# A perceiver's cross-attention on one core: value and key fills interleaved, and the next batch's context turned one tile per piece

## The reference, cut to what matters

```python
x, ctx_1024: (8, 128, 512), (8, 2048, 512)      # 16 heads of 64
q = einsum('btd,dhk->bthk', layernorm(x), Wq) + bq
k = einsum('bsd,dhk->bshk', ctx_1024, Wk) + bk
v = einsum('bsd,dhk->bshk', ctx_1024, Wv) + bv
probs = softmax(einsum('bshk,bthk->bhts', k, q / 8), axis=-1)
attn = einsum('bhts,bshk->bthk', probs, v)
x = x + einsum('bthk,hkd->btd', attn, Wo) + bo
```

## Time and profile before

| | us |
|---|---|
| three timed runs | 3320.79, 3321.17, 3326.48 |
| their median | 3321.17 |
| the profiled execution | 3323.82 |
| its span, first to last instruction | 3322.1 |
| PE busy (share of the span) | 3094.8 (93%) |
| DVE busy | 1755.2 (53%) |
| ACT busy | 1453.4 (44%) |
| mean granted PE clock | 0.930 |

### The profile page before, as it was taken

One profiled execution on the slowest core, in us unless ns is written; L12 is line 12 of the kernel. 1 busy time (PEld: TensorE's weight loads), 2 busy tenths in 40 slices (PEclk: granted clock), 3 DMA queues, 4 the chain that ended last, 5 costly groups with the idle time before them and its releaser, 6 DMA issues. The chain is left out here.

```text
span 3322.1 us, 62803 instructions
## 1 busy us (share of the span) xinstructions
PE 3094.8 (93%) x25686; PEld 2701.5 (81%) x25686; DVE 1755.2 (53%) x3257; ACT 1453.4 (44%) x2994; POOL 116.5 (4%) x87
## 2 busy tenths in 40 slices
PE   6899999999999999999999999999879679869997
PEld 5688888888888888888888888888736579859997
DVE  5355656565565555556555555655523788740001
ACT  3355555555555555555555555555512510011111
POOL 0000000000000000000000000000040320100001
PEclk9899999999999999999999999999989755579998
DMA  7311221121121112112112111211080000217761
GB/s 304 118 40 38 74 63 45 55 76 38 51 74 57 42 57 67 38 51 74 57 44 67 57 51 44 74 43 38 10 192 7 16 33 0 78 50 275 252 238 59
DMA packets 234789, 253.16 MB, mean 76 GB/s; under 512 B 22296, under 2 KB 169912, under 8 KB 234064
## 3 DMA queue, kind: packets, MB, share of 16 engines
q1 hardware_dynamic: 233008, 241.79, 22.8%
q0 software_dynamic: 1280, 4.20, 0.4%
q10 hardware_dynamic: 288, 4.19, 0.3%
HBM read 215.42 MB, written 34.70 MB: 75 GB/s over the span
## 5 line engine op out<-in xcount | busy, mean ns | idle before, releaser
L216 PE MATMUL fills<-wv_group,ctxT_hi 128*128 128x256 f32 x4096 | 799.5, 288 | 1.3 <-DVE ctxT_lo L421 0.6
L224 PE MATMUL fills<-ctxT_hi,wk_pairs 128*128 128x512 f32 x2048 | 704.9, 405 | 0.7 <-DVE keys L436 0.7
L216 PEld LDWEIGHTS fills<-wv_group,ctxT_hi 128*128 128x128 f32 x4096 | 655.3, 191 | 24.2 <-issue 21.0
L436 DVE SCALAR_TENSOR_TENSOR keys<-fills,bk,keys 64x512 fp32r<-64x512 f32 x512 | 383.8, 750 | 412.1 <-ACT keys L353 408.4
L216 PE MATMUL fills<-wv_group,ctxT_lo 128*128 128x256 f32 x2048 | 579.4, 283 | 0.0
L353 ACT ACTIVATE keys<-fills,bk 64x512 fp32r<-64x512 f32 x512 | 350.0, 684 | 408.3 <-PE fills L224 405.0
L224 PEld LDWEIGHTS fills<-ctxT_hi,wk_pairs 128*128 128x128 f32 x2048 | 387.8, 189 | 103.7 <-issue 23.8
L429 DVE TENSOR_TENSOR values<-fills,values 128x512 fp32r<-128x512 f32 x256 | 176.9, 691 | 435.7 <-ACT values L348 435.7
L224 PE MATMUL fills<-ctxT_lo,wk_pairs 128*128 128x512 f32 x1024 | 403.5, 394 | 0.0
L216 PEld LDWEIGHTS fills<-wv_group,ctxT_lo 128*128 128x128 f32 x2048 | 392.7, 192 | 0.0
L473 DVE TENSOR_TENSOR probsT<-probsT_ps,probsT 128x512 fp32r<-128x512 f32 x504 | 348.3, 691 | 66.3 <-ACT probsT L385 57.1
(11 more groups left out here) (211 smaller groups left out, 3105.5 us busy)
## 6 DMA issues: line engine op xcount, KB each, us to landing
e_w<-in_L_ffn_W SPq DMA_DIRECT2D x64, 1024.0 KB, 8.7
ctx_stage<-in_ctx SPq DMA_DIRECT2D x128, 256.0 KB, 2.9
wv_group<-wv_split SPq DMA_DIRECT2D x64, 512.0 KB, 4.6
wk_pairs<-wk_split SPq DMA_DIRECT2D x128, 256.0 KB, 3.2
q<-q_split SPq DMA_DIRECT2D x256, 64.0 KB, 2.7
q_split<-p_qb SPq DMA_DIRECT2D x16, 512.0 KB, 3.5
o_parts<-o_half SPq DMA_DIRECT2D x128, 64.0 KB, 1.5
a_ua<-o_parts SPq DMA_DIRECT2D x32, 256.0 KB, 6.6
```

The lines of the kernel that those rows point to most:

```text
L216: last = nc.tensor.matmul(pJ[:, bank[0], 256 * k:256 * k + 256], c[:, t, s:s + P], wv[:, w, t, :], start=t + n == 0, stop=t == DT - 1 and ...
L224: last = nc.tensor.matmul(pJ[:, bank[0], :], wk[:, p, w, t, :], c[:, t, 512 * j:512 * j + 512], start=t + n == 0, stop=t == DT - 1 and n == 2)
L436: last = nc.vector.scalar_tensor_tensor(out=keys[lo_rows(j), x, 512 * j:512 * j + 512], in0=pJ[DK * a:DK * a + DK, bk_, :], scalar=bk_sb[h ...
```

## The change

A group's fills come in the order V V K V V K V V K V V K K K K K: value fills at positions 0, 1, 3, 4, 6, 7, 9, 10 (`VALUE_AT`), the first pair's key fills at 2, 5, 8, 11 and the second pair's at 12 to 15 (`KEY_AT`). The 16 context tiles of the next batch are turned in pieces 45 to 57 (`CTX_AT`): two in 45, 46 and 57, one in each of the ten between. A piece's first tile is at the piece's start, as before; a second one, where there is one, between the scores and the fill. Numbers, banks and waits follow from the new tables by the same rules. On SP, the value weights of the next group but one are loaded after position 11, right ahead of the first pair's key weights (before: after position 7), and each context tile is loaded alone, behind the fill that frees its buffer. No matmul, evacuation or DMA is added or removed.

```diff
-    FIRST_CTX = 47
+    VALUE_AT = (0, 1, 3, 4, 6, 7, 9, 10)
+    KEY_AT = ((2, 5, 8, 11), (12, 13, 14, 15))
+    CTX_AT = (45, 45, 46, 46, 47, 48, 49, 50, 51, 52, 53, 54, 55, 56, 57, 57)
+
+    def work_of(pos):
+        if pos in VALUE_AT:
+            return 0, VALUE_AT.index(pos)
+        p = pos in KEY_AT[1]
+        return 1 + p, KEY_AT[p].index(pos)
+
+    def turns(m):
+        return [u for u in range(ST) if CTX_AT[u] == m]
 
     def fill_no(m, last=False):
-        return m if last else m + 2 * min(max(m - FIRST_CTX + 1, 0), ST // 2)
+        return m if last else m + sum(at <= m for at in CTX_AT)
 
     def ctx_no(u):
-        return FIRST_CTX + 3 * (u // 2) + u % 2
+        return CTX_AT[u] + u
...
 # SP
-                            k = 16 * g + 4 * i + j - FIRST_CTX
-                            if not last and 0 <= k < (ST - NS) // 2:
-                                sp.wait_ge(filled, PRO + PER * b + ctx_no(2 * k + 1) + 1)
-                                ctx_load(sp, b + 1, 2 * k + NS)
-                                ctx_load(sp, b + 1, 2 * k + NS + 1)
+                            for u in () if last else turns(16 * g + 4 * i + j):
+                                if u + NS < ST:
+                                    sp.wait_ge(filled, PRO + PER * b + ctx_no(u) + 1)
+                                    ctx_load(sp, b + 1, u + NS)
...
-                        if i and not (last and g >= 2):
+                        if i >= 2 and not (last and g >= 2):
                             sp.wait_ge(filled, PRO + PER * b + fill_no(16 * g + 4 * i + 3) + 1)
-                            if i == 1:
+                            if i == 2:
                                 wv_load(sp, (g + 2) % XG)
-                            else:
-                                wk_load(sp, (g + 2) % XG, i - 2)
+                            wk_load(sp, (g + 2) % XG, i - 2)
...
 # PE
+            def fill(no, seq, pos):
+                kind, n = work_of(pos)
+                if n == 0:
+                    pe.wait_ge(wk_in[kind - 1] if kind else wv_in, 32 * seq + 32)
                 pe.wait_ge(fill_lo, no - 1)
-                if i < 2:
-                    v_fill(seq, j, i)
+                if kind:
+                    k_fill(kind - 1, n)
                 else:
-                    k_fill(i - 2, j)
+                    v_fill(n)
...
-                            if turn:
-                                bank[0] = ctx_no(2 * k) % 2
-                                ctx_fill(PRO + PER * b + ctx_no(2 * k), b + 1, 2 * k)
+                            new = [] if last else turns(m)
+                            for u in new[0:1]:
+                                bank[0] = ctx_no(u) % 2
+                                ctx_fill(PRO + PER * b + ctx_no(u), b + 1, u)
...
-                            if turn:
-                                bank[0] = ctx_no(2 * k + 1) % 2
-                                ctx_fill(PRO + PER * b + ctx_no(2 * k + 1), b + 1, 2 * k + 1)
+                            for u in new[1:2]:
+                                bank[0] = ctx_no(u) % 2
+                                ctx_fill(PRO + PER * b + ctx_no(u), b + 1, u)
...
 # ACT
-                                if g and i < 2 and j == 0:
+                                pos = 4 * i + j
+                                if g and pos == VALUE_AT[0]:
                                     act.wait_ge(weighed, 64 * b + 16 * g)
-                                if i >= 2 and j == 0:
-                                    act.wait_ge(scored, 16 * b + 4 * g + 2 * (i - 2) + 2)
+                                for p in range(2):
+                                    if pos == KEY_AT[p][0]:
+                                        act.wait_ge(scored, 16 * b + 4 * g + 2 * p + 2)
```

More of the change, by code:

```diff
@@ L43, in cross_attention, with through @@
     PIECES = 16 * XG
-    FIRST_CTX = 47
     PRO = ST + 16
     PER = PIECES + ST
+    VALUE_AT = (0, 1, 3, 4, 6, 7, 9, 10)
[8 more added lines that the diff above has]
+        return [u for u in range(ST) if CTX_AT[u] == m]
     def fill_no(m, last=False):
-        return m if last else m + 2 * min(max(m - FIRST_CTX + 1, 0), ST // 2)
+        return m if last else m + sum(at <= m for at in CTX_AT)
     def ctx_no(u):
-        return FIRST_CTX + 3 * (u // 2) + u % 2
+        return CTX_AT[u] + u
+    def through(b, g, pos, last):
+        if g:
+            return PRO + PER * b + fill_no(16 * g - 16 + pos, last) + 1
+        return PRO + PER * (b - 1) + fill_no(16 * XG - 16 + pos) + 1 if b else ST + pos + 1
     es = ExitStack()
@@ L208, in ctx_fill, with v_fill @@
                 last.then_inc(filled, 1)
-            def v_fill(seq, j, i):
+            def v_fill(n):
                 for k in range(2):
-                    s = P * (2 * (4 * i + j) + k)
+                    s = P * (2 * n + k)
                     for t in range(DT):
-                        for n, (c, w) in enumerate(((ctx_hi, 0), (ctx_lo, 0), (ctx_hi, 1))):
+                        for a, (c, w) in enumerate(((ctx_hi, 0), (ctx_lo, 0), (ctx_hi, 1))):
                             last = nc.tensor.matmul(pJ[:, bank[0], 256 * k:256 * k + 256], c[:, t, s:s + P],
-                                                    wv[:, w, t, :], start=t + n == 0, stop=t == DT - 1 and n == 2)
+                                                    wv[:, w, t, :], start=t + a == 0, stop=t == DT - 1 and a == 2)
                 last.then_inc(filled, 1)
@@ L244, in score @@
                 pe.wait_ge(q_in[i], 128 * b + 32 * (g + 1))
-                pe.wait_ge(fill_lo, PER * b + (28 + 4 * (i // 2) if g == 0 else
-                                               PRO + fill_no(16 * g - 16 + 11 + 4 * (i // 2), last) + 1))
+                pe.wait_ge(fill_lo, through(b, g, KEY_AT[i // 2][3], last))
                 if h or not first[0]:
@@ L267, in transpose, with weigh @@
                 last.then_inc(transposed, 1)
-            def weigh(b, h, j):
+            def weigh(b, h, j, last):
                 g, i = h // 4, h % 4
@@ L274, in weigh @@
                     pe.wait_ge(o_copied, 16 * b + h + 1)
-                    pe.wait_ge(fill_lo, PER * b + (24 if g == 0 else PRO + fill_no(16 * g - 16 + 7) + 1))
+                    pe.wait_ge(fill_lo, through(b, g, VALUE_AT[7], last))
                 for k in range(4):
                     s = 4 * j + k
-                    last = nc.tensor.matmul(pO[:, 0:2 * P], values[:, g % 2, s, i, :],
+                    done = nc.tensor.matmul(pO[:, 0:2 * P], values[:, g % 2, s, i, :],
                                             probsT[:, j % 2, k, :, :].rearrange("p n t -> p (n t)"),
                                             start=s == 0, stop=s == ST - 1)
-                last.then_inc(weighed, 1)
+                done.then_inc(weighed, 1)
             first = [True]
@@ L302, in batch @@
                             if j:
-                                weigh(b, h, j - 1)
+                                weigh(b, h, j - 1, last)
                             elif h:
-                                weigh(b, h - 1, 3)
+                                weigh(b, h - 1, 3, last)
                             if more:
@@ L309, in batch @@
                                 score(b, h + 1, last)
-                            if turn:
-                                bank[0] = ctx_no(2 * k + 1) % 2
-                                ctx_fill(PRO + PER * b + ctx_no(2 * k + 1), b + 1, 2 * k + 1)
+                            for u in new[1:2]:
+                                bank[0] = ctx_no(u) % 2
+                                ctx_fill(PRO + PER * b + ctx_no(u), b + 1, u)
                             if more:
-                                bank[0] = fill_no(m) % 2
-                                fill(PRO + PER * b + fill_no(m, last), 4 * b + g + 1, i, j)
-                weigh(b, XH - 1, 3)
+                                bank[0] = fill_no(m, last) % 2
+                                fill(PRO + PER * b + fill_no(m, last), 4 * b + g + 1, 4 * i + j)
+                weigh(b, XH - 1, 3, last)
             for u in range(ST):
@@ L331, in _ @@
                 bank[0] = m % 2
-                fill(ST + m, 0, m // 4, m % 4)
+                fill(ST + m, 0, m)
             for b in range(batches - 1):
@@ L342, in fill_hi_ctx, with fill_hi_vk @@
                                pJ[:, bk_, :].rearrange("p (t s) -> p t s", t=DT)).then_inc(fill_hi, 1)
-            def fill_hi_vk(no, bk_, g, i, j):
+            def fill_hi_vk(no, bk_, g, pos):
+                kind, j = work_of(pos)
                 act.wait_ge(filled, no + 1)
-                if i < 2:
-                    n = 2 * (4 * i + j)
+                if not kind:
+                    n = 2 * j
                     nc.scalar.copy(values[:, g % 2, n:n + 2, :, 0:DK],
@@ L351, in fill_hi_vk @@
                 for a in range(2):
-                    x = 2 * (i - 2) + a
+                    x = 2 * (kind - 1) + a
```

(15 more changed lines are left out.)

23 lines of the change are left out of this document (8 added, 15 removed).

## The result

| | before | after |
|---|---|---|
| timed runs, median (range), us | 3322.78 (3320.79 to 3326.48) | 3359.77 (3358.33 to 3361.23) |
| ratio, 95% interval | | 1.011 (1.0093 to 1.0128) |
| span of the profiled execution, us | 3322.1 | 3359.5 |

The kernel became slower by 37.0 us. The forecast was 3362 us in a range of 3345 to 3390, and +40.8 us.

A forecast was written before the change was run, and what follows sets the result against it. PE's stream was taken as the bound. Per batch, 6.28 us more for context tiles less 0.48 for plain stops gave +5.80; seven batches, 40.6, plus 0.2 made +40.8 us, 3362 us, range 3345 to 3390.

The forecast's parts named there:

- PE's stream is the bound: Plain pieces: PE busy 66.03 of 66.26 us, so reordering fills only gives or takes PE's short stops.
- Plain groups: Groups without context tiles: stops after key fills total 1.38 us a group in place of 1.30, +0.08.
- the stop behind position 2: Plain groups: a value fill follows the key fill at position 2, and the stop costs 0.22 us.
- The context stretch: Pieces 45 to 57: fills wait for the bank of the fill before; tiles cost 19.62 us a batch, 6.28 more.
- SP's order, the weight loads: SP's reordered tile and weight loads still land in time: cost nothing; lost cover would cost 3.2 to 4.6 us each.
- The clock: Context stretch: four drops of 1.58 us kept, piece 46 of the new order having the form of 47.
- The rival that more long stops bring more drops: Context stretch: six more drops +9.5 us, 3372, or 31 more +49, 3411; chance of over ten additional 0.12.
- The sum: Whole kernel: seven batches at 5.80 us, 40.6, and 0.2 for the last batch: +40.8 us, 3362 us.
- The spread that pays: Context stretch: single tiles without waits cost 6.7 us a batch, 46 us faster in all, 3275; chance 0.05.
- The cancelling: Context stretch: four waits of 2.45 us fall to about 1.0, so the time stays at 3321; chance 0.07.

The follow-up runs named there:

- the moved tiles: The change with its context tiles placed two each in pieces 45, 46, 49, 50, 52, 53, 55 and 57: 3301.28 us, 0.9956 of the kernel before.
- two stops taken away: The change with the tile of piece 51 moved to 52 and that of 54 to 53: 3325.70 us, 1.0026 of the kernel before.
- the order alone: The change's new order of fills with the old turn, two context tiles in each of pieces 47 to 54: 3349.44 us, 1.0096 of the kernel before.

## Why the prediction was right, point by point

**PE's stream is the bound.** Right: six forecasts worked out from PE's stops, of 10 to 64 us, were met to within 8.

**Plain groups.** Forecast +0.08 us a group; the sixteen pieces of batch 0's second group take 300.43 - 232.35 = 68.08 us before [300.43 in rows 3] and 300.20 - 232.00 = 68.20 after, by the starts of their first instructions, +0.12. The other three starts, first of the kernel before, then of the kernel after:

```profile
232.35 0.65 PE L279 MATMUL o_ps<-probsT,values 128*128 128x256 f32 x4
```

```profile
232.00 0.64 PE L292 MATMUL o_ps<-probsT,values 128*128 128x256 f32 x4
...
300.20 0.64 PE L292 MATMUL o_ps<-probsT,values 128*128 128x256 f32 x4
```

One term was mis-sized: the stop behind position 2 costs 0.19 + 0.10, not 0.22, because the chain took 249.22 - 245.25 = 3.97 and not 3.90. ACT and DVE each started a few hundredths later on that key fill.

**The context stretch.** Forecast 19.62 us a batch for the tiles. From the rows above: 47 pays 6.07 - 3.67 = 2.40, 48 6.22 - 3.78 = 2.44, 51 6.21 - 3.78 = 2.43 (forecast 2.45 each); 52 pays 4.54 - 3.78 = 0.76 (0.82), 46 6.80 - 3.67 = 3.13 (3.08). In a batch without a drop of the clock the tiles cost 19.5 us after the change and 13.4 before. The step on which all hung was that a single tile moves the bank by two from fill to fill, so that the fill takes over the second tile's wait. It stands in the trace as the change of the waiting instruction from L206 to L231 and L239. This is the rule of the Trainium skill, Perfetto Trace Analysis, section Matmuls (let groups rotate through banks), broken by a count of tiles; the rule and the trace of the kernel after agree: the tile of piece 47, in the other bank, starts at the key fill's end (368.62), the fill in the same bank 3.19 us later. Not run were single tiles at the same places with a bank of their own, which would part the bank from the place.

**SP's order, the weight loads.** Put at nothing, and it was: the key weights take longer to land after the change (4.3 us median on the page, 3.2 before), where SP issues them right behind the value weights; but the moved tiles have the same order of loads (4.8 us) and are the faster kernel. In no piece does PE wait for them.

**The clock.** Forecast four drops, and there were four: three in piece 46, one in piece 48 (7.46 us at 0.81). That the number came out is partly luck. The prediction told piece 47 from 48 by two stands of PE against one, but its rows show one stand of 1.76 us in each; piece 48, forecast to have none behind a single stop, had one; and the same piece 46 had none in the trace of the moved tiles and two in that of the two stops taken away. The rival that more long stops bring more drops did not come about in the change, with 35 of them in place of 14, but in part with the order alone, nine drops at 28. Each of these counts is from one profiled execution. Of the rule of the Trainium skill, TensorE: Matmul & The Clock Gate, section A second HAM failure mode (short idle times between groups make the clock go back and forth), the traces bear out this much: all 19 drops in the turns of these traces fall in pieces with one of the long stops (1.7 to 1.8 us). That more such stops bring more drops is neither borne out nor ruled out.

**The sum.** +40.8 forecast for the pieces, 40.2 measured. The total of 37.0 is smaller by what the forecast held fixed: 0.5 us ahead of the first `weigh`, and the last group behind the fills. Busy time of that group, transposes of the probabilities to last `weigh`, before:

```profile
2375.89:2411.64 35.75, 27.82 (x156) 21.95 (x156) 19.46 (x31) 18.64 (x44) 0.00 (x0) 0.86 0.03 8
```

and after:

```profile
2415.62:2449.57 33.95, 26.51 (x156) 20.52 (x156) 19.41 (x31) 18.53 (x44) 0.00 (x0) 0.90 0.03 8
```

The same 156 matmuls take 1.80 us less at a mean granted clock of 0.90 in place of 0.86. Nothing in them was changed, and why the clock fell less often in this stretch was not tried; in the traces of the six experiments the same stretch takes some 32 to 34.5 us at 1.00 to 0.90, so these 1.80 us need not come from the change.

**The rivals.** The spread that pays would have needed the next fill within 1.3 us; it started after 3.19. The cancelling would have needed about 1.0 us for a wait that took 2.4.

## What to carry to other kernels

Where two buffers alternate by a running number, an item put between two others moves the parity: look at which item now has the same buffer as the one just ahead of it, and price that item's evacuation against the work between them. Put inserted work where the item ahead leaves quickly, or where something long stands between, rather than evenly. And where a chain of two engines with two instructions each sets the stop, let the second engine start on the first half: this one signal was worth 57 us in the kernel before, where the best placement tried was worth 18.

## What the runs showed of the hardware that was not expected

PE's clock fell after some stops and not after others that look alike. With two tiles behind a key fill, piece 47 had a drop in 4 of 7 turns before and in 2 of 7 with the order alone, piece 46 in 3 of 7 after the change, in 2 of 7 with two stops taken away and in 0 of 7 with the moved tiles, at the same length of 6.8 us without a drop and the same 5.0 us of PE work; piece 48 with its pair had none in 14 turns, and pieces 51 and 54, of the same make and nearly the same length, had seven in 14 with the order alone. A drop costs some 1.5 us (7.46 against 6.22 in piece 48, and 0.27 more in the next). With the stops 0.7 shorter (PE busy 5.01 of 6.08 us) no turn of three kernels had any. What tells the stops with a drop from those without stays open.
